# Selective scan of a Mamba layer: the D-skip term, the residual add and the last sum of a block move to other engines and places

## What is computed

```python
def step(h, inp):
    u_t, d_t, b_t, c_t = inp
    dA = jnp.exp(d_t[..., None] * A)
    dBu = (d_t * u_t)[..., None] * b_t[:, None, :]
    h = dA * h + dBu
    y = jnp.einsum('bdn,bn->bd', h, c_t)
    return (h, y)
...
return y + u * D_skip              # end of the scan
...
y = y * jax.nn.silu(z)
out = y @ out_proj_w.T
...
x = x + layer0(_gn(x))             # the residual, then layer 1
```

## Time and profile before

| what | value |
|---|---|
| median of 3 executions | 5207.64 us (5202.15 to 5208.96) |
| the profiled execution | 5205.0 us; its span, first to last instruction, 5203.0 us |
| first and last scan instruction | 1221.2 us and 4037.8 us |
| mean granted clock of TensorE | 0.976 |
| busy over the whole span | PE 92%, PEld 58%, DVE 79%, ACT 55%, POOL 64% |

### The profile page before, as it was taken

One profiled execution on the slowest core, in us unless ns is written; L12 is line 12 of the kernel. 1 busy time (PEld: TensorE's weight loads), 2 busy tenths in 40 slices (PEclk: granted clock), 3 DMA queues, 4 the chain that ended last, 5 costly groups with the idle time before them and its releaser, 6 DMA issues. The chain is left out here.

```text
span 5203.0 us, 121297 instructions
## 1 busy us (share of the span) xinstructions
PE 4779.7 (92%) x47928; PEld 3025.2 (58%) x47928; DVE 4124.5 (79%) x4332; ACT 2874.5 (55%) x5942; POOL 3333.1 (64%) x1648
## 2 busy tenths in 40 slices
PE   5999999965999999999999999999999699999899
PEld 4666666643455545545555555455555488888687
DVE  7888888856999989989999999899999477776432
ACT  2666666645666656656666666666665344554211
POOL 0577777766988878878888888888888122222000
PEclk9999999987999999999999999999999899999999
DMA  4334443333323232323233223222331111111443
GB/s 197 119 143 151 146 146 139 142 134 115 93 77 87 86 89 75 89 79 91 75 91 91 82 83 90 83 79 86 91 91 58 53 73 73 73 74 80 192 178 146
DMA packets 191792, 538.47 MB, mean 103 GB/s; under 512 B 15825, under 2 KB 15841, under 8 KB 181841
## 3 DMA queue, kind: packets, MB, share of 16 engines
q1 hardware_dynamic: 185920, 480.31, 28.1%
q0 software_dynamic: 5104, 51.35, 2.5%
q10 hardware_dynamic: 288, 0.00, 0.0%
HBM read 329.22 MB, written 202.38 MB: 102 GB/s over the span
## 5 line engine op out<-in xcount | busy, mean ns | idle before, releaser
L917 POOL TENSOR_TENSOR sc_hc<-sc_hc,sc_c_rep 128x1024 f32<-128x1024 f32 x1024 | 2388.6, 2370 | 465.3 <-ACT sc_state L926 463.4
L1139 DVE TENSOR_TENSOR_SCAN sc_hc<-sc_da,sc_state,sc_ring 128x512 f32<-128x512 f32 x2048 | 2444.9, 1261 | 221.8 <-PE sc_ring L1033 188.9
L953 ACT ACTIVATE sc_da<-sc_delta,l_neg_a 128x512 f32<-128x512 f32 x2048 | 1352.6, 708 | 0.0
L1033 PEld LDWEIGHTS sc_ring<-sc_diag,sc_dut 64*64 64x64 f32 x32768 | 906.4, 133 | 563.7 <-issue 549.3
L1033 PE MATMUL sc_ring<-sc_diag,sc_dut 64*64 64x128 f32 x32768 | 1101.0, 275 | 48.1 <-DVE sc_hc L1139 24.7
L1041 PE MATMUL sc_y_ps<-sc_hc,sc_fold 128*64 128x512 f32 x4096 | 996.6, 607 | 94.7 <-POOL sc_hc L917 94.7
L1041 PEld LDWEIGHTS sc_y_ps<-sc_hc,sc_fold 128*64 128x64 f32 x4096 | 249.1, 136 | 569.9 <-issue 442.4
L1347 POOL TENSOR_TENSOR l_count<-l_count,as_oh 128x1024 f32<-128x1024 f32 x64 | 182.4, 2850 | 508.2 <-DVE as_oh L1530 508.2
L1063 PE MATMUL sc_o_ps<-sc_yg,sc_w_out 128*128 128x512 f32 x1024 | 504.6, 617 | 2.9 <-ACT sc_x_res L946 2.1
L926 ACT ACTIVATE sc_state<-sc_hc 128x2 f32<-128x2 f32 x1024 | 204.8, 200 | 489.8 <-DVE sc_hc L1139 489.4
L71 PE MATMUL fr_mm<-fr_xn_hi,l0f_w_in_hi 128*128 128x512 f32 x1024 | 438.0, 428 | 26.3 <-DVE fr_delta L671 11.8
(11 more groups left out here) (169 smaller groups left out, 6488.8 us busy)
## 6 DMA issues: line engine op xcount, KB each, us to landing
sc_duz<-spill SPq DMA_DIRECT2D x128, 768.0 KB, 6.1
sc_delta<-spill SPq DMA_DIRECT2D x256, 256.0 KB, 4.1
spill<-fr_z SPq DMA_DIRECT2D x64, 512.0 KB, 2.8
spill<-fr_u SPq DMA_DIRECT2D x32, 1024.0 KB, 8.7
spill<-fr_du SPq DMA_DIRECT2D x32, 1024.0 KB, 4.3
spill<-fr_delta SPq DMA_DIRECT2D x32, 1024.0 KB, 6.4
sc_c_rep<-bc SPq DMA_DIRECT2D x128, 256.0 KB, 4.0
soft<-as_et SPq DMA_DIRECT2D x16, 2048.0 KB, 6.3
```

The lines of the kernel that those rows point to most:

```text
L917: nc.gpsimd.tensor_tensor(hc[:, p], hc[:, p], c_rep[:, 2 * q:2 * q + 2, :], ALU.mult).then_inc(s_hp, 1)
L953: nc.scalar.activation(da[:, p % 4, r, :], delta[:, i % 2, p % 2, :], ACT.Exp, scale=keep.neg_a[:, c:c + 1]).then_inc(s_da, 1)
L1033: done = nc.tensor.matmul(to[:, :, k::4], dut[rows, i % 2, k, HALF * h:HALF * h + HALF], diag[rows, u, 4 * q + c:4 * q + 4:2, k, :], start ...
L1139: nc.vector.tensor_tensor_scan(hc[:, p, r, :], da[:, p % 4, r, :], ring[:, SLOT[at], r::2], state[:, i, 2 * p + r:2 * p + r + 1], ALU.mult ...
```

## The change

Six things are done together, all in `scan`:

1. D times u is written into `y_ps` by ScalarE (`write_skip`) right behind `keep_turned` at p=5. The matmuls of `add_skip` and the weights `skip` with their eight set-up instructions on VectorE are gone. `add_up` 0 waits for the write.
2. The residual matmuls (L1069) are gone. ScalarE copies `o_ps` to a new two-buffer tile `o_sb` (`keep_projection`, where `x1_sum` was), and GpSimd adds it onto `x_res` (`add_x`), behind its multiply of pair 3 in the even blocks.
3. `statistics` on VectorE, at its old place behind pair 4, now waits for GpSimd's add.
4. TensorE does `add_up` 3 of the block before ahead of fill 3 instead of behind it.
5. Of the two projections ahead of `turn` one goes behind it.
6. `turn_b` goes ahead of the projection and of `turn`; `keep_column` goes ahead of `keep_turned`; for i=1 `turn` waits for the kept column. The transposes of `turn` become one accumulation group over the bank.

```diff
@@ gpsimd, body @@
                         nc.gpsimd.tensor_tensor(hc[:, p], hc[:, p], c_rep[:, 2 * q:2 * q + 2, :], ALU.mult).then_inc(s_hp, 1)
+                        if p == 3 and i in (2, 4, 6) and past:
+                            add_x(g - 1, i // 2 - 1)
+                        if p == 3 and i == 0 and len(past) > 1:
+                            add_x(g - 2, KC - 1)
+
+            def add_x(g, m):
+                pool.wait_ge(s_x[m % 2], 32 * g + 16 * (m // 2) + 16)
+                pool.wait_ge(s_o, KC * g + m + 1)
+                nc.gpsimd.tensor_tensor(x_res[:, m % 2, :], x_res[:, m % 2, :], o_sb[:, m % 2, :], ALU.add).then_inc(s_sum, 1)
@@ scalar @@
-            def x1_sum(g, m):
+            def keep_projection(g, m):
                 act.wait_ge(s_op, KC * g + m + 1)
-                nc.scalar.activation(x_res[:, m % 2, :], o_ps[:], ACT.Copy).then_inc(s_sum, 1)
+                before = KC * g + m - 1
+                if begun(before):
+                    act.wait_ge(s_sum, before)
+                nc.scalar.activation(o_sb[:, m % 2, :], o_ps[:], ACT.Copy).then_inc(s_o, 1)
+
+            def write_skip(g, i, turned):
+
+                if turned:
+                    act.wait_ge(s_dut, KD * g + i + 2)
+                else:
+                    act.wait_ge(s_yg, KD * g + i)
+                act.wait_ge(s_duz[i % 4], 16 * (KD // 4 * g + i // 4 + 1))
+                nc.scalar.activation(y_ps[:], duz[:, i % 4, 1, :], ACT.Copy, scale=keep.dskip[:, i:i + 1]).then_inc(s_seed, 1)
...
                         if p == 5:
+                            if i == 0 and more:
+                                keep_column(g + 1)
                             if i + 1 < KD:
                                 keep_turned(g, i + 1)
                             elif more:
                                 keep_turned(g + 1, 0)
-                            if i == 0 and more:
-                                keep_column(g + 1)
+                            write_skip(g, i, i + 1 < KD or more)
@@ tensor @@
             def add_up(g, i, q):
                 pe.wait_ge(s_hp, pairs(g, i, 2 * q + 1))
+                if q == 0:
+                    pe.wait_ge(s_seed, KD * g + i + 1)
...
                 if last == KD:
-                    pe.wait_ge(s_x[m % 2], 32 * g + 16 * (m // 2) + 16)
-                    pe.sem_inc(s_free, 1)
-                    for h in range(2):
-                        rows = slice(HALF * h, HALF * h + HALF)
-                        done = nc.tensor.matmul(o_ps[rows, :], fold[rows, :], x_res[rows, m % 2, :], start=False, stop=True)
                     done.then_inc(s_op, 1)
...
-                    fill(g, u, i, 3)
                     if i:
                         add_up(g, i - 1, 3)
                     elif past:
                         add_up(g - 1, KD - 1, 3)
+                    fill(g, u, i, 3)
                     fill(g, u, i, 4)
-                    if past:
-                        project(g - 1, 1 - u, i // 2, half, half + 2)
-                    if follows:
-                        turn(nxt[0], nxt[2])
-                    fill(g, u, i, 5)
                     if i == 0 and more:
                         turn_b(g + 1)
-                    add_skip(g, i, follows, i == 0 and more)
+                    if past:
+                        project(g - 1, 1 - u, i // 2, half, half + 1)
+                    if follows:
+                        turn(nxt[0], nxt[2], g + 2 if more else g + 1)
+                    if past:
+                        project(g - 1, 1 - u, i // 2, half + 1, half + 2)
+                    fill(g, u, i, 5)
                     add_up(g, i, 0)
@@ vector @@
             def statistics(b, j, m):
                 g = b * NJ + j
-                dve.wait_ge(s_sum, KC * g + m + 1 + 1)
+                dve.wait_ge(s_sum, KC * g + m + 1)
```

More of the change, by code:

```diff
@@ L917, in body @@
                         nc.gpsimd.tensor_tensor(hc[:, p], hc[:, p], c_rep[:, 2 * q:2 * q + 2, :], ALU.mult).then_inc(s_hp, 1)
+                        if p == 3 and i in (2, 4, 6) and past:
[6 more added lines that the diff above has]
+                nc.gpsimd.tensor_tensor(x_res[:, m % 2, :], x_res[:, m % 2, :], o_sb[:, m % 2, :], ALU.add).then_inc(s_sum, 1)
             chunks(pool, body)
+            add_x(NG - 2, KC - 1)
+            for m in range(KC):
+                add_x(NG - 1, m)
         @block.scalar
@@ L975, in body @@
                         if p == 1 and i in (2, 4, 6) and past:
-                            x1_sum(g - 1, i // 2 - 1)
+                            keep_projection(g - 1, i // 2 - 1)
                         if p == 1 and i == 0 and len(past) > 1:
-                            x1_sum(g - 2, KC - 1)
+                            keep_projection(g - 2, KC - 1)
                         if i and more:
@@ L992, in _, with turn @@
                 keep_state(NG - 1, KD - 1, p)
-            x1_sum(NG - 2, 3)
+            keep_projection(NG - 2, 3)
             for m in range(KC):
-                x1_sum(NG - 1, m)
+                keep_projection(NG - 1, m)
         @block.tensor
         def _(pe):
-            def turn(g, i):
+            def turn(g, i, column=1):
                 pe.wait_ge(s_duz[i % 4], 16 * (KD // 4 * g + i // 4 + 1))
@@ L1004, in turn @@
                     pe.wait_ge(s_yg, before)
+                if i == 1:
+                    pe.wait_ge(s_col, column)
                 for k in range(4):
-                    done = nc.tensor.transpose(y_ps[:, k * P:k * P + P], duz[:, i % 4, 0, k::4], keep.ident[:])
+                    done = nc.tensor.matmul(y_ps[:, k * P:k * P + P], duz[:, i % 4, 0, k::4], keep.ident[:], is_transpose=True,
+                                            start=(k == 0), stop=(k == 3))
                 done.then_inc(s_turn, 1)
@@ L1010, in turn_b @@
                 pe.wait_ge(s_row, 16 * g + 16)
-                pe.wait_ge(s_dut, KD * g - KD + 2 if begun(g) else 1)
+                before = KD * (g - 1)
+                if begun(before):
+                    pe.wait_ge(s_yg, before)
                 pe.sem_inc(s_free, 1)
@@ L1041, in add_up @@
                         done = nc.tensor.matmul(y_ps[HALF * h:HALF * h + HALF, :], fold[:], hc[:, 2 * q + h, r, :],
-                                                start=False, stop=(q == 3 and r == 1))
+                                                start=False, stop=(q == 3 and r == 1), skip_group_check=True)
                 done.then_inc(s_acc, 1)
[L1045 to L1052, removed]
-                pe.sem_inc(s_free, 1)
-                for h in range(2):
-                    rows = slice(HALF * h, HALF * h + HALF)
-                    nc.tensor.matmul(y_ps[rows, :], skip[rows, i, :], duz[rows, i % 4, 1, :], start=True, stop=False)
             def project(g, u, m, first, last):
                 for i in range(first, last):
-                    if i == 0:
-                        pe.wait_ge(s_sum, KC * g + m + 1)
-                    nc.tensor.matmul(o_ps[:], w_out[:, i, m * P:(m + 1) * P], yg[:, u, i, :], start=(i == 0), stop=False)
-                if last == KD:
-                    pe.wait_ge(s_x[m % 2], 32 * g + 16 * (m // 2) + 16)
-                    pe.sem_inc(s_free, 1)
-                    for h in range(2):
-                        rows = slice(HALF * h, HALF * h + HALF)
-                        done = nc.tensor.matmul(o_ps[rows, :], fold[rows, :], x_res[rows, m % 2, :], start=False, stop=True)
+                    before = KC * g + m
+                    if i == 0 and begun(before):
+                        pe.wait_ge(s_o, before)
+                    done = nc.tensor.matmul(o_ps[:], w_out[:, i, m * P:(m + 1) * P], yg[:, u, i, :],
+                                            start=(i == 0), stop=(i == KD - 1))
+                if last == KD:
                     done.then_inc(s_op, 1)
@@ L1103, in body @@
                         fill(*nxt, 2)
+            turn_b(0)
+            pe.wait_ge(s_col, 1)
             turn(0, 0)
-            pe.wait_ge(s_skip, KD + 1)
-            turn_b(0)
+            pe.wait_ge(s_fold, 1)
             pe.wait_ge(s_w, 16)
-            pe.wait_ge(s_col, 1)
             for p in range(3):
@@ L1119, in _ @@
         def _(dve):
[L1120 to L1123, removed]
+            nc.vector.tensor_tensor(fold[:], keep.ident[:, 0:HALF], keep.ident[:, HALF:P], ALU.add).then_inc(s_fold, 1)
             def before(b):
```

11 lines of the change are left out of this document (6 added, 5 removed).

## The result

The changed kernel takes 5247.93 us (median of 4 runs, 5239.72 to 5252.29), the kernel before in the same session 5204.90 (4 runs, 5198.72 to 5208.96): a ratio of 1.0082, 95% interval 1.0063 to 1.0100. It is slower by 0.8%, and 0.9 us above the forecast. The profiled execution took 5251.86 us, with a span of 5250.2.

What follows compares the result with a forecast made beforehand. A ring of waits over PE, ACT and POOL (turn, kept state, pair 2, `add_up` 1) was taken as the bound. Even blocks +87.8, blocks 0 +16.5 and -0.9, odd -60.0, ends -4.0: +39.4, so 5247 us; range 5180 to 5300.

Steps and rivals of the forecast that it cites:

- (a): Skip matmuls removed from PE: 0.97 us between turn and `add_up` 1, where PE waits anyway; worth nothing, the wait grows.
- (c): One projection behind turn on PE: 0.91 us leaves the 15.22 from `add_up` 1 to the next turn, making 14.31.
- (e): `add_up` 3 ahead of fill 3: same PE work, POOL's pair 7 needed one fill earlier, 4.69 us from its start to turn.
- (b): write_skip on ACT, ahead of keep_state: POOL's pair 2 comes at T+2.2 instead of T+1.44, T being the start of turn.
- (f): add_x on POOL ends 8.19 us behind turn; DVE's statistics wait about 4 us for it; even block 23.35 us, 1.95 more.
- (g): Block 0 of a chunk: turn_b ahead of turn costs 0.56 us; with add_x 23.91, 1.18 more than now.
- (h): Chunk 0: gate to gate over the ring 19.04 us, still under DVE's 19.35, so nothing.
- (i): Start of the scan: diagonals begin about 0.5 us behind the start of keep_turned instead of 1.84: -1.3.
- (j): End of the scan: slices about 7.8 us instead of 8.84 without the residual, last slice's add 1.3 more: -2.7 in all.
- A: Rival: the statistics' wait does not set the pace, POOL's queue makes the even block 22.26 us; 5183 us, chance 0.12.
- B: Rival: PE's queue is the bound, both kinds of block take 19.68 us; 4935 us, chance 0.05.
- C: Rival: dearer pieces on the ring, PSUM write doubled (+71) or add_x at 2.07 us (+48); 5295 to 5318 us, chance 0.17.

Runs made afterwards that it cites:

- write alone: Kernel before, with the skip written by ACT instead of PE's matmuls; `turn_b`, `keep_column` and start order as in the changed kernel: 5303.36 us, ratio 1.0181.
- projection alone: Kernel before, with one of the two projections ahead of turn put behind it: 5118.50 us, ratio 0.9834.
- The first two experiments: Changed kernel with statistics behind pair 7: 5176.91 us; changed kernel with add behind pair 7, statistics behind pair 4 of the next odd block: 5123.93 us.
- the experiment with add and statistics moved: Changed kernel, with the add behind pair 7 and the statistics behind pair 4 of the odd block that follows: 5123.93 us, ratio 0.9835.
- the early sum alone: Kernel before, with `add_up` 3 of the block before ahead of fill 3, nothing else: 5192.37 us, ratio 0.9978.
- the kept state before the write: Changed kernel, with pair 2's state kept between keep_turned and write_skip, nothing else: 5151.99 us, ratio 0.9901.
- the first experiment: Changed kernel, with VectorE's statistics behind pair 7 of the even blocks instead of pair 4: 5176.91 us, ratio 0.9949.
- the last run: Changed kernel, with TensorE's wait for the output projection's weights behind the first three fills: one execution, 5256.93 us.

## Why the prediction was right, step by step

- **(a), (c), (d), (e), odd blocks: right.** Forecast 21.25, measured 21.31 from turn to turn. The wait before `add_up` 1 grew to 1.49 us (forecast near 1.5): the 0.97 us of matmuls taken off PE went into that wait. The write alone and the projection alone confirm both signs: +98 us (some 34 of them by the clock, not by the ring) and -87.
- **(b) the write: right.** T+2.20 for POOL's pair 2, exactly as forecast; the write took 0.69 us, 0.63 to the next instruction. That is a decay's price (0.708 in the earlier trace rows), not keep_turned's. "ScalarE: Activation LUTs" of the Trainium skill, section "Step-by-step: what each stage is for", says that ScalarE writes faster to PSUM than to SBUF; here the difference is 0.02 us, so the sum by the row was the one to use.
- **(f) add and statistics: right, the main term.** Even blocks 23.43, forecast 23.35. DVE stood still for 3.98 us (forecast about 4), statistics came at T+8.24 (T+8.19), `add_up` 3 at T+18.69 (T+18.66). The gates do not alternate at 23.4 and 21.2, as the prediction's signs had it, but at about 24.1 and 20.7; the turns do. The add took 1.26 us, not the earlier trace rows's 2.07, but in this kernel DVE stands still during it, which says nothing of a shared port. "SBUF — State Buffer" of the Trainium skill, section "SBUF: two separate sides", would have the add undisturbed also while DVE reads one source from PSUM. The first two experiments agree: there DVE is busy all through the 60 adds, and they take 1.28 us in the median.
- **(g) block 0: mis-sized.** From gate to gate 24.75, which is 0.70 above an even block, not 0.56. Small: 2 us.
- **(h) chunk 0: wrong, +6 us where I said nothing.** I took 0.75 us from gate to turn, as it was. But fills 3 and 4 now stand between `add_up` 3 and turn when there is no projection, one more than before by (e), so it is 1.79:

```profile
1268.67 1.98 PE L1064 MATMUL sc_ring<-sc_diag,sc_dut 64*64 64x128 f32 x64
1270.58 0.75 PE L1034 MATMUL sc_y_ps<-keep_ident,sc_duz 128*128 128x128 f32 x4
```

 The gate there starts at 1268.79. 1.79 + 2.2 + 14.06 + 0.05 + 1.98 = 20.08, over DVE's 19.35, and the first gates are 20.11 apart. In the experiment with add and statistics moved, where chunk 0 runs the same work, six in a row are; in the changed kernel the next are 21.76, 19.34 and 21.48, two of them with a sum at half clock (below). The write alone (19.34), the early sum alone (19.37) and the kept state before the write (19.36) each stay at DVE's pace: it takes both edits at once. My sum had the write in it, but not what (e) does to the way from gate to turn.
- **(i) the start: wrong.** -1.3 forecast, -0.3 measured (25.50 us for 25.80), which is inside the spread of that stretch. The diagonals did come 1.1 us earlier, but PE's first fill waited for the load of the output weights (row below). It had done so before too: that load landed 23.39 us behind DVE's first instruction and the fill began at 23.53, though its 16 diagonals were done at 12.18. It did not show, because the first decays came later still and the scan waited for them:

```profile
1221.20 4.12 PE L1064 MATMUL sc_ring<-sc_diag,sc_dut 64*64 64x128 f32 x72 [16.79 <-DMA sc_w_out<-in_w_out]
```

- **(j) the end: right.** From the last gate to the next stage 37.00 us instead of 39.70: -2.7.
- **The loop ends: left at +-10, in fact -12.7.** The last sum first, alone, took 9 off them, so step (e) has a part in it that I had not seen. The rest is not shown: the same loop code cost 3.1 us more in the last run's trace, and one kernel with the fill first had cheap jumps as well.

The spans differ by 47.2 us (5250.2 - 5203.0). The sum had 39.4. To it come, from gate to gate, 6.0 for chunk 0, 0.4 for the block 0 behind it, 9.2 for the other blocks of chunks 1 to 15 (0.14 us a pair of ordinary blocks, a little more with a block 0), 3.9 for the first and the last block of chunk 15 (+2.72 and +1.40, where the sum has +1.18 and -1.00), 1.0 at the start, and -12.7 at the loop ends: 47.2. (Ahead of the scan the two traces differ by +2.4 us and behind it by -2.5, which cancels.) So the forecast is good in its main terms, but that the total came within 0.9 us is luck: some 20 us of terms that were too small or missing met 12.7 at the loop ends. In the medians the difference was 43.0.

Of the rivals, A names what would be left if the statistics' wait were not there, and the first experiment shows just that (22.18 for the even block, 22.26 by A's sum). B's 19.68 is nearly reached (19.9) only when all three hold-ups are taken away, and pair 3's state with them. C's prices did not come: the write took 0.69 us, the add 1.26 to 1.28.

## What to carry to other kernels

Count an edit against the ring of waits that sets the pace, not against the busiest engine: here 0.97 us of work taken off the busiest engine gained nothing, 0.63 put onto one that was mostly idle cost 0.75 a block, and the same instruction one place further down cost nothing that could be seen. An instruction that waits for another engine holds all that stands behind it in its queue, so a short consumer of a late result (here the statistics) belongs where its input is sure to be done, even a whole block later. After breaking a ring, look for the next instruction that would close it, and cost edits that share a bound together.

## What was not expected of the hardware

- **TensorE's granted clock fell inside a steady loop.** In the write alone, 21 blocks had one `add_up` at 0.53 of the clock, 3.63 us instead of 1.94, after waits of 0.47 and 1.82 us with 2.98 us of work between. The changed kernel, with a wait of 1.5 us and no such second one ahead of it, keeps 1.00 in chunks 1 to 15 except at the loop ends and at the very end. In its chunk 0, where blocks have waits of 0.47 and 1.83 again, three sums fell too, two of them right behind such a pair. Here is the first, and the clock during it (columns as above):

```profile
1317.85 3.59 PE L1074 MATMUL sc_y_ps<-sc_hc,sc_fold 128*64 128x512 f32 x8 [1.83 <-POOL sc_hc L919]
```

```profile
1317.80:1321.40 3.60, 3.55 (x12) 0.72 (x12) 2.45 (x3) 3.02 (x8) 3.60 (x2) 0.53 0.00 0
```

 An added wait can so cost more than its length; the runs do not tell from which point on.
- **A loop's jump costs 3 to 10 us, and not the same with every order of its body.** The second jump cost 10.2 us before (fill first) and 4.7 in the changed kernel (sum first); part of the 10.2 is again the clock (0.50 from 2276 to 2285). But in the write alone it cost 5.3 with the fill first, so the order is not the whole cause, and the rest stays open.
